# V of an attention block transposed by VectorE and moved by small SBUF transfers instead of transposed by TensorE

## The reference

```python
h = group_norm(x)                                   # 32 groups, no affine
q = bn(conv1x1(h, qw)); k = bn(conv1x1(h, kw))      # 8 heads, 32 channels each, 196 pixels
v4 = bn(conv1x1(h, vw))                             # 1024 channels: 8 heads of 128
vl = bn(depthwise_conv3x3(v4, lvw))
a = einsum('bhid,bhjd->bhij', q, k) * SCALE + bias
a = softmax(mix_heads(a, th1w, th1b))
a = mix_heads(a, th2w, th2b)
o = einsum('bhij,bhjd->bhid', a, v)                 # needs V with pixels on the contraction side
out = x + bn(conv1x1(relu(o + vl), pw))
```

## Time and profile before

| | us |
|---|---|
| median of 3 runs | 4813.25 |
| lowest and highest | 4812.56, 4814.12 |
| profiled execution | 4811.84 |
| its span, first to last instruction | 4810.0 |
| TensorE matmul busy in the span | 4779.1 |
| VectorE busy | 4175.9 |
| ScalarE busy | 3251.4 |
| GpSimd busy | 988.6 |

### The profile page before, as it was taken

How to read it: one execution, slowest core, us unless ns; L and a number is a source line. 1 busy time by engine, 2 the same in 40 slices (tenths; PEclk the granted TensorE clock), 3 DMA queues, 4 the chain that set the end, 5 groups by cost and what they waited for, 6 DMA issues and landing times.

```text
span 4810.0 us, 111468 instructions
## 1 busy us (share of the span) xinstructions
PE 4779.1 (99%) x35842; PEld 4760.2 (99%) x35842; DVE 4175.9 (87%) x10897; ACT 3251.4 (68%) x8005; POOL 988.6 (21%) x1093
## 2 busy tenths in 40 slices
PE   7999999999999999999999999999999999999999
PEld 7999999999999999999999999999999999999999
DVE  8888888889888898888888988889888888898887
ACT  6666666666667666667666666766666766666665
POOL 3212212121121221221212212122121221221211
PEclk9999999999999999999999999999999999999999
DMA  1000000000000000000000000000000000000000
GB/s 57 26 20 30 19 26 30 15 30 25 20 30 15 30 25 20 30 15 30 30 15 30 25 20 30 15 30 25 20 30 15 30 29 16 30 21 24 30 15 26
DMA packets 55148, 120.23 MB, mean 25 GB/s; under 512 B 3650, under 2 KB 5842, under 8 KB 55124
## 3 DMA queue, kind: packets, MB, share of 16 engines
q1 hardware_dynamic: 55124, 119.93, 7.4%
HBM read 81.38 MB, written 38.54 MB: 25 GB/s over the span
## 4 chain that ended last, share of the span: by engine, by line
PE 98%; DVE 1%; issue 0%; DMA 0%; ACT 0%; SPq 0%; DVEq 0%
PE psA L250 43%; PE psA L399 14%; PE psL L250 12%; PE psM L250 10%; PE psM L377 8%; PE psL L377 6%; PE psM L367 2%; PE psL L367 2%; DVE psC L620 1%; PE psA L268 0%; PE psA L263 0%; DMA qa<-in_wqkv 0%; DVE probs L675 0%; DVE x_lo L601 0%; DVE q_lo L650 0%
## 5 line engine op out<-in xcount | busy, mean ns | idle before, releaser
L620 DVE SCALAR_TENSOR_TENSOR psC<-vpad,par,psC 128x406 f32<-128x406 f32 x3072 | 1808.7, 637 | 0.0
L498 ACT ACTIVATE probs<-probs,nmax 112x196 f32<-112x196 f32 x1792 | 799.0, 449 | 649.0 <-DVE nmax L675 641.8
L250 PE MATMUL psA<-x_hi,w_lo 128*128 128x392 f32 x2304 | 795.0, 345 | 8.5 <-DVE x_lo L601 8.5
L250 PE MATMUL psA<-x_lo,w_hi 128*128 128x392 f32 x2304 | 788.9, 342 | 0.0
L250 PE MATMUL psA<-x_hi,w_hi 128*128 128x392 f32 x2304 | 788.1, 342 | 0.0
L399 PE MATMUL psA<-qa,shared 105*128 105x196 f32 x4096 | 693.9, 330 | 3.0 <-DVE shared L719 3.0
L399 PEld LDWEIGHTS psA<-qa,shared 105*128 105x128 f32 x4096 | 680.2, 191 | 3.3 <-DVE shared L719 3.3
L650 DVE SCALAR_TENSOR_TENSOR q_lo<-q,th,q_hi 128x392 fp32r<-128x392 f32 x1024 | 604.4, 621 | 34.6 <-ACT q_hi L442 27.6
L719 DVE TENSOR_TENSOR shared<-psA,shared 128x392 f32<-128x392 f32 x512 | 290.1, 567 | 366.5 <-PE psA L399 366.5
L442 ACT ACTIVATE q_hi<-q,th 128x392 fp32r<-128x392 f32 x1024 | 582.0, 620 | 6.0
L434 ACT ACTIVATE o_hi<-shared 128x392 fp32r<-128x392 f32 x512 | 271.5, 530 | 457.6 <-DVE shared L719 457.6
(11 more groups left out here) (85 smaller groups left out, 10500.0 us busy)
## 6 DMA issues: line engine op xcount, KB each, us to landing
xs<-in_x SPq DMA_DIRECT2D x64, 588.0 KB, 3.8
shared<-in_x SPq DMA_DIRECT2D x64, 588.0 KB, 3.8
out<-shared SPq DMA_DIRECT2D x63, 588.0 KB, 3.0
qa<-in_wqkv SPq DMA_DIRECT2D x3, 768.0 KB, 6.7
stage_wp<-in_wp SPq DMA_DIRECT2D x1, 1536.0 KB, 9.9
out<-shared SPq DMA_DIRECT2D x3, 196.0 KB, 2.0
shared<-in_abx SPq DMA_DIRECT2D x1, 165.4 KB
par<-in_par SPq DMA_DIRECT2D x1, 70.5 KB
```

The lines of the kernel that those rows point to most:

```text
L250: last = nc.tensor.matmul(dst, w, r, start=(begin and n == 0), stop=(end and n == 2))
L498: nc.scalar.activation(row, row, ACT.Exp, bias=nmax[:, img, b:b + 1], scale=-1.0, accum_out=rowsum[:, img, b:b + 1]).then_inc(s_exp, 1)
L620: nc.vector.scalar_tensor_tensor(a if tap == 7 else sums, src, taps[:, c, TAPS[tap]:TAPS[tap] + 1], a if tap == 0 else sums, MUL, ADD).the ...
```

## The change

V is no longer transposed on TensorE. After the last logits of a pair are read, VectorE transposes V of each image with one instruction in blocks of 32 channels by 32 keys (`turn(0)`, `turn(1)`): 128 x (8 heads x 7 blocks of keys x 32), 1792 elements on a partition, into a new buffer `turned`. A block stays on its 32 partitions, so the keys of block b of channel group a come to lie on partitions 32a to 32a+31. SyncE then issues 28 transfers an image from SBUF to SBUF (7 blocks of keys x 4 channel groups), each of 32 partitions x 8 heads x 32 elements (32 KB in runs of 128 bytes), which put the blocks into `vt` with the keys on the partitions. AV of an image waits for all 28 of its transfers.

With the V uses gone, TensorE's and ScalarE's list has 14 uses, all mix; `x_hi` of the next pair is made after use 6. The two chunks of an image are now keys 0 to 95 and 96 to 209; the mix makes 114 rows for each chunk, and AV uses 96 and 114 of them.

`turned` has no place of its own: it lies over `x_lo`, `q`, `k_hi` and `k` in a buffer `front`. Image 0's part covers `x_lo` and most of `q`, image 1's the rest. So GpSimd makes the next pair's `x_lo` only after all 28 transfers of image 0 have landed. On SP, the 56 transfers stand between the load of the next x and the store of the pair before.

```diff
+            def move_turned(t, img):
+                sp.wait_ge(s_turned, 2 * t + img + 1)
+                for b in range(BLOCKS):
+                    jc, row = (0, b * BLK) if b * BLK < CUT else (1, b * BLK - CUT)
+                    for a in range(P // BLK):
+                        sp.dma_start(vt[row:row + BLK, img, jc, :, a * BLK:(a + 1) * BLK],
+                                     turned[a * BLK:(a + 1) * BLK, img, b, :, :]).then_inc(s_vt_in[img], 16)
             def step(t, first, last):
                 if not last:
                     sp.wait_ge(s_xhi, t + 1)
                     sp.wait_ge(s_xlo, t + 1)
                     load_x(t + 1)
+                for img in range(2):
+                    move_turned(t, img)
                 if not first:
                     store(t)
                 residual(t + 1)
...
-                for use in range(22):
-                    img, (what, n) = use // 11, USES[use % 11]
-                    bank_free(use)
-                    if what == "vt":
-                        jc, cg = divmod(n, 2)
-                        for c in range(4):
-                            at_ = PITCH + 1 + img * PITCH * PITCH + jc * HALF
-                            mm = nc.tensor.transpose(mix_bank(use)[:, c * P:(c + 1) * P],
-                                                     vpad[:, 4 * cg + c, at_:at_ + HALF], ident[:, :])
-                        mm.then_inc(s_vt_mm, 1)
+                for use in range(14):
+                    img, n = divmod(use, 7)
...
                 for img in range(2):
-                    pe.wait_ge(s_vt_sb, 8 * t + 4 * img + 4)
+                    pe.wait_ge(s_vt_in[img], 16 * MOVES * (t + 1))
                     pe.wait_ge(s_mix_sb, 14 * t + 7 * img + 7)
...
+                def turn(img):
+                    at_ = PITCH + 1 + img * PITCH * PITCH
+                    nc.vector.transpose(turned[:, img, :, :, :].rearrange("p b c k -> p c b k"),
+                                        vpad[:, :, at_:at_ + BLOCKS * BLK].rearrange("p c (b k) -> p c b k", b=BLOCKS)
+                                        ).then_inc(s_turned, 1)
...
-                convs(3)
+                turn(0)
                 dve.wait_ge(s_exp, 28 * t + 28)
                 nc.vector.reciprocal(rinv[:, 1, :], rowsum[:, 1, :]).then_inc(s_rinv, 1)
-                convs(3)
+                turn(1)
...
-                    pool.wait_ge(s_v_mm, VT * (t + 1))
+                    wait_alone(pool, s_vt_in[0], 16 * MOVES * (t + 1))
                     x_low(t + 1)
```

More of the change, by code:

```diff
@@ L18 @@
 PITCH = RES + 1
-HALF = RES // 2 * PITCH
+KEYS = RES * PITCH
+BLK = 32
+BLOCKS = -(-KEYS // BLK)
+CUT = 3 * BLK
+REST = KEYS - CUT
+PART = VT * BLK
 HR = P // KD
@@ L29 @@
 EPS = 1e-5
+Q_AT = 2 * CT * PIX
+K_HI_AT = Q_AT + QT * COLS
+K_AT = K_HI_AT + QT * COLS
 GAP = 2 * RES * QT * HP - VT // 2 * ACC - 4 * DH
@@ L76, in build @@
         x_hi = sb("x_hi", [P, 2, CT, PIX], f32r)
[L77 to L82, removed]
+        x_lo = over("x_lo", [P, 2, CT, PIX])
+        k_hi = over("k_hi", [P, QT, COLS], K_HI_AT)
+        k_lo = over("k_lo", [P, QT, COLS], K_AT)
+        front = sb("front", [P, 2 * BLOCKS * PART])
         q_hi = over("q_hi", [P, 2 * RES, QT, HP])
         qa = sb("qa", [P, 4 * RES * HP])
-        probs = sb("probs", [P, 2, RES, 2 * HALF])
+        probs = sb("probs", [P, 2, RES, KEYS])
         nmax = sb("nmax", [HP, 2, RES])
@@ L106, in build @@
         acc = shared[:, 0:vt_at].rearrange("p (c n) -> p c n", c=VT)
-        vt = shared[:, vt_at:vt_at + 4 * DH].rearrange("p (i j n) -> p i j n", i=2, j=2)
+        vt = shared[:, vt_at:vt_at + 4 * DH].rearrange("p (i j c n) -> p i j c n", i=2, j=2, c=VT)
         res = shared[:, res_at:].rearrange("p (i k n) -> p i k n", i=2, k=CT)
@@ L111, in build @@
         kron1 = shared[0:HP, vt_at + WINDOW:vt_at + WINDOW + HP].rearrange("p (g i) -> p g i", g=NH)
-        attn = qa[0:HALF, :].rearrange("p (i j g n) -> p i j g n", i=2, j=2, g=NH)
+        q = front[:, Q_AT:K_HI_AT].rearrange("p (k n) -> p k n", k=QT)
+        k = front[:, K_AT:K_AT + QT * COLS].rearrange("p (k n) -> p k n", k=QT)
+        turned = front[:, :].rearrange("p (i b c n) -> p i b c n", i=2, b=BLOCKS, c=VT)
+        attn = qa[0:REST, :].rearrange("p (i j g n) -> p i j g n", i=2, j=2, g=NH)
         stage_w = qa[:, 0:CT * 12 * P].rearrange("p (k m) -> p k m", k=CT)
@@ L183, in mix_bank @@
         def mix_bank(use):
-            return (psM if use % 4 < 2 else psL)[0:HALF, use % 2, :]
+            return (psM if use % 4 < 2 else psL)[0:REST, use % 2, :]
         def t_has_next(t):
@@ new lines, in step @@
+                    else:
+                        pe.wait_ge(s_mix_sb, 14 * t + use - 3)
+                    pe.wait_ge(s_exp, 28 * t + 14 * img + 2 * n + 2)
+                    pe.wait_ge(s_mixw, 8 * t + 4 * img + group(2 * n + 1) + 1)
+                    bank = mix_bank(use)[:, 0:4 * HP].rearrange("p (j g b i) -> p j g b i", j=2, g=NH, b=2)
+                    for jc in range(2):
+                        for b in range(2):
+                            mm = nc.tensor.matmul(bank[:, jc, :, b, :],
+                                                  probs[0:HP + 1, img, 2 * n + b, jc * CUT:jc * CUT + REST],
+                                                  mixw[0:HP + 1, img, 2 * n + b, :].rearrange("p (g i) -> p g i", g=NH),
+                                                  start=True, stop=True)
@@ L382, in step @@
+                    mm.then_inc(s_mix_mm, 1)
                 if first:
@@ L397, in step @@
                             g = 2 * n + e
-                            for jc in range(2):
+                            for jc, rows in enumerate((CUT, REST)):
                                 mm = nc.tensor.matmul(psA[:, u % 2, e * PIX:(e + 1) * PIX],
-                                                      vt[0:HALF, img, jc, g * D:(g + 1) * D], attn[:, img, jc, g, :],
+                                                      vt[0:rows, img, jc, g, :],
+                                                      attn[0:rows, img, jc, g, :],
                                                       start=(jc == 0), stop=(jc == 1))
@@ L502, in step @@
                         conv_centre(t, CENTRES[n])
[L503 to L516, removed]
+                for use in range(14):
+                    img, n = divmod(use, 7)
+                    act.wait_ge(s_mix_mm, 14 * t + use + 1)
+                    if use == 0 and not first:
+                        act.wait_ge(s_av_mm, 8 * t)
+                    src = mix_bank(use)[:, 0:4 * HP].rearrange("p (j g m) -> p j g m", j=2, g=NH)
+                    nc.scalar.copy(attn[:, img, :, :, 2 * n * RES:(2 * n + 2) * RES], src).then_inc(s_mix_sb, 1)
+                    if use == 6 and not last:
                         act.wait_ge(s_v_mm, VT * (t + 1))
```

34 lines of the change are left out of this document (7 added, 27 removed).

## The result

The changed kernel takes 6154.81 us (median of 4 runs), the kernel before 4813.45 us in the runs beside it: ratio 1.2786, 95% interval 1.2764 to 1.2808. The profiled execution has a span of 6150.5 us. That is slower, as forecast, but by 1341 us where 492 us were forecast, and above the range's end of 5950 us.

The account below looks back on a forecast made before the run. The SP queue's issuing of 56 moves was to bound the kernel: 5.3 us lateness plus 2.3 us clock loss, 7.7 us a pair with rounding, 82.2 in place of 74.5 us; forecast 5305 us, range 4920 to 5950 us.

Parts of the forecast that it names:

- The issue of a move: SP queue: 0.44 us each, 56 take 24.6 us, so V of image 1 is late and AV ends 5.3 us later.
- The clock: TensorE on image 1's AV: half clock after idling, costing 2.3 us a pair, between 0 and 2.7.
- The start of the moves: SP queue: `turn(0)` starts at the four taps at 2456.80 and ends about 2458.8, when the 56 issues begin.
- The transposes: VectorE: 2.0 us each, 4.0 us for two; bounds 1.0 and 6.7 us each.
- the second limit: VectorE alone before AV's additions: about 75.1 us a pair, TensorE's gain already gone; not the binding limit.
- 114 stationary rows at nothing: TensorE's mix uses: 114 stationary rows in place of 105 cost nothing, 14 uses staying at 0.77 us each.
- What was held to be hidden: GpSimd and SP queue: `x_lo`, store, residual and next x load cost nothing; x hidden by some 4 us.
- (c): DMA transfers do not keep up with the issues: at 0.8 us a move, about 6600 us; chance 17%.
- (a): SP queue issues a move in 0.34 us or less, VectorE's additions set the end: 75.1 us a pair, 4850 us; 6%.
- (b): SP issues at 0.30 us or less and VectorE transposes at 1.0 us each: 71.0 us a pair, 4586 us; 3%.
- the case in which the two cancel: Whole kernel: TensorE's gain and the added costs just cancel, time within 0.2% of before; chance 3%.
- (d): TensorE keeps its clock over the wait for V: 5155 us, within the forecast's own range; chance 10%.

Follow-up runs that it names:

- the run with enough fillers: Changed kernel plus filler matmuls on TensorE while it waits for V, 38 ahead of image 0's AV and 74 ahead of image 1's: 5961.64 us, ratio 1.2386.
- the run with few moves and `x_lo` held back: Changed kernel with two transfers an image in place of 28 (V not in order), `x_lo` waiting until VectorE is past tap 50 of 64: 4973.33 us.
- the mixed version: Changed kernel, but image 0 transposed by TensorE, image 1 by VectorE and 16 moves: 4734.37 us; with image 0 in chunks of 105 keys again, 4720.64 us.

## Why the prediction was wrong

The mechanism was right: V of image 1 comes late because the SP queue cannot issue 56 moves in time, and TensorE loses its clock over the wait. The size was not. The forecast had 7.7 us a pair, measured are 21.1. By its terms:

**The issue of a move, mis-sized.** The step that failed is "so I take 0.44 us": 56 x 0.44 = 24.6 us forecast, 36.63 us measured, 12.0 of the missing 13.4 us. All the issues in the rows of before are between HBM and SBUF; none is from SBUF to SBUF. I chose the row that is nearest in the number of runs, and the runs hardly matter: eight times fewer saved 3%, twice as many cost 3%. What matters is that both ends are in SBUF: 0.59 us in place of 0.42 for the same 32 partitions and runs of 1 KB. My upper end of 0.65 us held, to the digit, but no row stood behind that either (it lay under the 0.71 us of one load), and the range was then cut at 0.60 us and so at 5950. With 0.65 us the same sum gives 7.7 + 56 x 0.21 = 19.5 us a pair, about 6060 us. The clock and the start of the moves, 0.9 and 0.6 us a pair, are most of what is then left.

**The clock, right in kind, small in size.** 2.3 us forecast, bounded at 2.7; 3.0 us by the run with enough fillers, 8.43 - 5.2 = 3.2 us by the trace. The bound came from one spell behind which TensorE needed 5.3 us to be back; here it works at half clock from 3067.3 to about 3073.8 us, 6.5 us.

**The start of the moves.** The four taps at 2456.80 hold one that is still in front of `turn(0)` in the code, so the moves start 0.6 us later than I had them.

**The transposes.** 2.0 us forecast by a line through two rows, 2.01 us measured. That was in part luck: any two rows lie on one line, and neither was of a transpose. The third row, 4392 ns, from which the upper bound of 6.7 us was made, is hardly a pace of VectorE's. The timelines of GpSimd and VectorE in the first pair of the kernel before:

```profile
13.52 4.18 POOL L770 TENSOR_TENSOR w_lo<-qa,w_hi 128x1536 fp32r<-128x1536 f32 x1 [3.80 <-ACT w_hi L416]
14.55 4.39 DVE L601 TENSOR_TENSOR x_lo<-xs,x_hi 128x1176 fp32r<-128x1176 f32 x1
```

GpSimd is done at 17.70 us and VectorE 1.24 us later, about what 1176 elements cost at 1.04 ns each. The other price that the prediction gives, 4.4 us for one transpose, does not hold here. The landing: 1.6 us after an issue's end forecast, 1.56 measured.

**The sum.** 5.3 + 2.3 is 7.6; the 7.7 adds a tenth that no step has, 6 us in all. The range begins at 4920 us, above its own lower end of 4900. Neither bears on the result.

**The next limit.** 75.1 us a pair for VectorE alone; the pairs with the clock kept took 74.7 in the run with few moves and `x_lo` held back. But what the forecast called the second limit has two companions that it did not see: the clock that is lost when TensorE waits for VectorE, up to 3.3 us, and the collision with GpSimd's `x_lo`, 2.3 us, which comes only once V is in time.

**114 stationary rows at nothing.** They cost 14 x 0.03 = 0.4 us a pair; hidden in the changed kernel, where TensorE waits anyway, and worth 13.7 us in all for one image of the mixed version.

**What was held to be hidden.** `x_lo`, the store, the residual and the load of x: all are, by the trace of the pair shown. VectorE's statistics start without a wait although the load of x took 5.0 us in place of 3.8.

**The rivals.** (c), transfers that do not keep up, falls: the DMA engines are 34% busy during the moves. Its time, 6600 us, is nearest to the measured one of the cases named for a slower result, but for a reason that does not hold. That none of a transfer's fixed time overlaps, 112 us a pair, is out as well: all 56 had landed 38.2 us after the first was issued. (a), (b) and the case in which the two cancel fall with the price of an issue. (d) falls: the clock was lost.

## What to carry to other kernels

Price a plan of many small transfers by their number first, and by an issue with the same two ends; bytes, runs and partitions come after. Joining two in one gave back 1092 of 1341 us here. And where two engines can both do a job and one of them is full, give the second as much of it as it has slack: VectorE had 3.3 us and one image cost it 2.0, both images 4.0; one image wins 1.9%, and both lose 3.3% even with four moves and `x_lo` held back. An engine with slack is worth no more than that slack, and when TensorE has to wait for it the clock is lost on top.

## What the runs showed of the hardware that I had not expected

- An issue from SBUF to SBUF takes the queue 0.58 to 0.61 us back to back and 0.52 us alone, for 4 to 128 partitions and 4 to 32 KB; from HBM to SBUF it is 0.42 to 0.43 for 32 and 128 partitions. SP and ScalarE issue side by side at the full rate of each.
- A VectorE instruction with both tensor operands in SBUF that started beside a GpSimd instruction with two SBUF operands was not slowed evenly: it ended 0.44 us behind the other's end, as if it had stood until then (2.97 us in place of 0.6). In pair 32 of the kernel before the same happened on a small scale: the tap at 2422.35 took 0.86 us, and ended 0.44 us behind GpSimd's `k_lo` (`2421.74 1.03 POOL L777 TENSOR_TENSOR k_lo<-k,k_hi 128x392 fp32r<-128x392 f32 x1`). Beside `x_lo`, taps with their second operand in PSUM took 0.64 us as always.
- A 32 x 32 transpose of 32-bit data on VectorE runs at one element in 1.12 ns when it writes runs of 32, and 3573 ns for 1792 elements, 1.8 times as long, when it writes every eighth element.
- Behind one and the same idle spell of 2.98 us TensorE's clock was kept in some pairs and fell to half in others, so that pairs of 74.7 and 77.6 us stand in one run. Behind the spells of 5 us and more that are shown here it fell each time; in the first pair of the kernel before it fell behind 2.14 us.
